# A linear-attention layer's two programs run as one, with the experts' weight pieces dealt out by step

## The chip, the cores and the metric

One core of a Trainium2 chip. The time is the device's microseconds for the whole kernel (two layers); the lower the better. Beside it stands one execution taken by the hardware profiler, whose span and rows are quoted here. VectorE is DVE in the rows, ScalarE is ACT, GpSimd is POOL, TensorE is PE (its weight loads PEld), and SP is the engine that issues most transfers.

## The reference, cut to what matters

2 x 1024 tokens of 512 numbers go through attention, a ternary feed-forward layer, a linear-attention layer and 16 experts of which each token takes two, each with a residual and a layer norm. The part that is changed:

```python
q = k = x @ Wqk + bqk
v = silu(x @ Wv + bv); u = silu(x @ Wu + bu)
q, kh, vh = elu(heads(q)), elu(heads(k)), heads(v)
kv  = einsum('bhnd,bhne->bhde', kh, vh)      # over all 1024 rows of a batch
out = einsum('bhnd,bhde->bhne', q, kv)
out = u * layernorm(out, ln_g, ln_b)
x   = layernorm(x + out @ Wo + bo)
logits = x @ gate_w.T                        # of the experts' router
```

An expert has a gate and up weight of 512 x 704 and a down weight of 352 x 512, all float32.

## The kernel before, in words

Tokens are in 16 tiles of 128 rows (`NT`), 8 to a batch (`TB`). Each product is made from float16 high and low halves: three products for one. Each phase is a program of its own, with its own semaphores, and each engine's order in it is written out by hand: `unrolled(n, stages)` takes steps 0, 1, 2, ... and in each step goes through a list of (lag, function) and calls the function for tile step - lag. An engine does its list in order, so a wait in one function holds up all that stand behind it.

`ternary_ffn` (from L1004) runs 18 steps and more: per tile 32 matmuls at L1084 and 32 at L1094, with the hidden rows turned by a transfer (L1062) that SP issues, and it makes the high and low halves of the next layer's weights (L1144, L1210).

`linear_features` (from L1344) makes, per tile, z = x @ (Wqk, Wv, Wu) in three PSUM banks (L1337, bias L1341), exp and two tanh on ScalarE (L1434, L1439), relu, e, v and U on VectorE (L1485 to L1492), one subtraction on GpSimd (L1530), then the key-value product summed in PSUM over a batch (L1411), the turned keys (L1417) and their halves (L1443, L1497). U of all 16 tiles is kept.

`linear_output_and_route` (from L1536) starts when that program is over. Per tile: q (L1602), its statistics and gating on VectorE (L209, L1690, L1694), the root of the variance (L220), the product with U (L1723) and the low half (L1729) on GpSimd, turning (L164, evacuated at L1654), @ Wo in TensorE (L1337 with `out_ps_y`), residual and statistics on VectorE (L1701, L209), root and shift on GpSimd (L1742, L1745), norm and halves (L1659, L1667, L1736), turning again (L1671), and the logits (L1631, L1709).

`ExpertSplit` (from L1239) turns the experts' float32 weights to float16 halves in the chip's memory. A piece is one k-chunk: seven to an expert, four of 128 x 704, two of 128 x 512 and one of 96 x 512. SP loads it (L1275, L1280) to a ring of buffers, ScalarE makes the high half (L1312), VectorE the low half (L1317), SP stores both (L1290). In `linear_features` the ring has six buffers, the transfers run freely (`transfers`), and the halves of 14 experts (98 pieces) are spread evenly over the steps (`spread`). `linear_output_and_route` takes the last two experts and seven pieces of the shared one, in a ring of four.

Of the kernel before, what the change touches and what calls it, by code (L numbers as in the profile page):

```python
# [1004 lines left out]
def ternary_ffn(nc, m, d):  # L1005
# [8 lines left out]
    with Phase(nc, "ffn") as f:  # L1014
# [27 lines left out]
        ht_in = [[f.sem(f"ht_in{u}{part}") for part in range(2)] for u in range(2)]  # L1042

        with f.block() as block:  # L1044
            @block.sync
            def _(sp):
# [54 lines left out]
            def _(act):  # L1101
# [39 lines left out]
                def next_high(t):  # L1141
# [5 lines left out]
                                      (4, of_layer(h_norm)), (1, of_layer(next_high))])  # L1147

            @block.vector
            def _(dve):  # L1150
# [56 lines left out]
                def next_low(t):  # L1207
# [7 lines left out]
                                      (1, of_layer(x_norm)), (1, of_layer(next_low))])  # L1215
# [19 lines left out]
LIN_EXPERTS = 14  # L1235


class ExpertSplit:
# [54 lines left out]
    def transfers(self, sp):  # L1293

        lag = self.ring - 2
        for i in range(self.count + lag):
            if i < self.count:
                self.load(sp, i)
            if i >= lag:
                self.store(sp, i - lag)  # L1300

# [18 lines left out]
    def spread(self, fn, eng, tiles, later=0):  # L1320


        def until(t):
            return self.count if t == tiles else max(0, t * self.count // tiles - later)

        def at(t):
            if t < tiles:
                for i in range(until(t), until(t + 1)):
                    fn(eng, i)
        return at  # L1330
# [13 lines left out]
def linear_features(nc, m, d):  # L1344

    with Phase(nc, "lin") as f:
# [4 lines left out]
        ps_x = [f.ps(f"ps_x{u}", [P, 2, KC, P], F16) for u in range(2)]  # L1356
        ps_z = [f.ps(f"ps_z{n}", [P, D], F32) for n in range(3)]
        ps_kv = [f.ps(f"ps_kv{b}", [P, KC, P], F32) for b in range(B)]
        ps_k = f.ps("ps_k", [P, KC, P], F32)
        brow = m.U[0:LO_ROW + 1, NT - 4:NT, :]  # L1360
# [6 lines left out]
        split = ExpertSplit(f, m, d, 6, 0, LIN_EXPERTS, 0)  # L1367
        with f.block() as block:
            @block.sync
            def _(sp):  # L1370
                sp.wait_ge(b_zero, 1)
                for i, n in enumerate(("bqk", "bv", "bu", "bo")):
                    sp.dma_start(brow[0:LO_ROW + 1:LO_ROW, i, :], d[f"L1_attn_{n}"][None, :].to_broadcast([2, D])).then_inc(b_in, 16)
                split.transfers(sp)
                for i, n in enumerate(("ln_g", "ln_b")):
                    sp.dma_start(m.ln_gb[:, i, :], d[f"L1_attn_{n}"][None, :].to_broadcast([P, D])).then_inc(m.gb_in, 16)
                split.wait_stored(sp)

            @block.tensor
            def _(pe):  # L1380
                def xt(t):
# [4 lines left out]
                    after(pe, xt_evac, t - 1 - AHEAD)  # L1386
                    transpose_parts(pe, ps_x[u], x2[u], m).then_inc(xt_done, 1)

                def z(t):
                    u = t % 2  # L1390
                    after(pe, xt_evac, t + 1 - AHEAD)
                    if t == 0:
                        for n in range(3):
                            weighed(pe, m, ps_z[n][:, :], n, xT[u])
                        pe.wait_ge(ones_done, 1)
                        pe.wait_ge(bl_done, 1)
                        for n in range(3):
                            biased(pe, m, ps_z[n][:, :], n).then_inc(z_done, 1)
                        return
                    for n, sem in enumerate((relu_done, v_done, u_done)):  # L1400
                        after(pe, sem, t)
                        weighed(pe, m, ps_z[n][:, :], n, xT[u])
                        biased(pe, m, ps_z[n][:, :], n).then_inc(z_done, 1)

                def kv(t):
                    u = t % 2
                    pe.wait_ge(k_done, t + 1)
                    pe.wait_ge(v_done, t + 1)
                    for g in range(KC):
                        s = slice(g * P, (g + 1) * P)  # L1410
                        last = pe.matmul(ps_kv[t // TB][:, g, :], relu[u][:, s], tanh[u][:, 0, s],  # L1411
# [8 lines left out]
                unrolled(NT, [(1, xt), (2, z), (3, kv)])  # L1420

            @block.scalar
            def _(act):
# [6 lines left out]
                def nonlinear(t):  # L1430
                    u = t % 2
                    after(act, k_done, t - 1)
                    act.wait_ge(z_done, t * 3 + 1)
                    act.activation(e[u][:, :], ps_z[0][:, :], ACT.Exp, scale=1.0 / WS).then_inc(e_done, 1)  # L1434
                    after(act, u_done, t - 1)
                    after(act, kv_done, t - 1)
                    for n in range(2):
                        act.wait_ge(z_done, t * 3 + 2 + n)
                        act.activation(tanh[u][:, n, :], ps_z[1 + n][:, :], ACT.Tanh, scale=0.5 / WS).then_inc(tanh_done, 1)  # L1439

                def kt_hi(t):
                    act.wait_ge(kt_done, t + 1)
                    act.activation(m.kT[:, 0, :, t * P:(t + 1) * P], ps_k[:, :, :], ACT.Copy).then_inc(kth_done, 1)  # L1443

                def kv_hi(t):
# [4 lines left out]
                    for a in range(4):  # L1450
                        s = slice(a * DL, (a + 1) * DL)
                        act.activation(m.kv[s, t // TB, 0, :, s], ps_kv[t // TB][s, :, s], ACT.Copy,
                                       scale=KV_SCALE / (2 * WS)).then_inc(kvh_done, 1)

                def biases(t):
                    if t == 0:
# [3 lines left out]
                unrolled(NT, [(0, lambda t: xhi(t + 1)), (1, biases), (2, nonlinear), (3, kt_hi), (3, kv_hi),  # L1460
                              (1, split.spread(split.high, act, NT, 3))])

            @block.vector
            def _(dve):
                dve.memset(m.kv[:, :, :, :, :], 0.0).then_inc(zero_done, 1)

                def biases(t):
                    if t == 0:
                        dve.wait_ge(bh_done, 1)
                        dve.scalar_tensor_tensor(m.bias[low_row, :, :], m.U[low_row, NT - 4:NT, :], WS, m.bias[low_row, :, :],  # L1470
# [1044 lines left out]
```

## Time and profile before

| | |
|---|---|
| median of 3 runs | 1739.52 us (1738.38 to 1745.71) |
| the profiled execution: its time, its span | 1740.19 us, 1738.4 us |
| busy share: PE, DVE, ACT, POOL | 91%, 68%, 54%, 33% |
| mean granted clock of TensorE | 0.973 |
| ternary layer ends, features start | 906.9 us into the span |
| features end, output starts | 1099 us |
| output ends, the experts' program starts | 1211 us |

Busy shares are averages over stages with different limits. The stage in question is the stretch from 907 to 1211 us; a wait of an engine counts where nothing else hides it. Idle time is printed in brackets behind a row, with what released the engine.

### The profile page before, as it was taken

To read this page: it belongs to the slowest core of one execution; us is meant where nothing else is said; L and a number is where in the kernel's file an instruction comes from. 1 tells how busy PE (TensorE), PEld (TensorE's weight loads), DVE (VectorE), ACT (ScalarE), POOL (GpSimd) and SP (SyncE) were. 2 spreads that over 40 slices of the span, in tenths; PEclk is the share of its full clock that TensorE was granted. 3 is DMA by queue.
4 is the path that set the end of the run, shared out by engine and by line. 5 is a ranking of instruction groups with operands and counts; after the bars stand their busy time and mean duration, and the time that the engine had idled before them with its cause. 6 is when DMAs were issued, how large, how long until landed. Compare 5 with 4: busy or idle time off the path is not lost. (4 is left out here: it accounts for less than half of the span.)

```text
span 1738.4 us, 33564 instructions
## 1 busy us (share of the span) xinstructions
PE 1585.8 (91%) x12554; PEld 803.7 (46%) x12554; DVE 1176.6 (68%) x2074; ACT 933.9 (54%) x1641; POOL 576.3 (33%) x583
## 2 busy tenths in 40 slices
PE   6899999889999997999978999687898899999997
PEld 3533333364333342444434444454555556666564
DVE  4599998468999955899857777895723243333387
ACT  5756777345677754767736665476223333333332
POOL 4556575161000021223321111595271111111265
PEclk9999999899999998999999999798999999999999
DMA  7323332000000002655638999551151764456344
GB/s 248 137 39 56 76 68 48 2 1 2 14 2 2 2 2 63 125 109 110 106 73 315 353 334 363 179 182 61 55 101 51 276 226 167 154 179 219 105 126 134
DMA packets 177842, 211.42 MB, mean 122 GB/s; under 512 B 114203, under 2 KB 117625, under 8 KB 175505
## 3 DMA queue, kind: packets, MB, share of 16 engines
q1 hardware_dynamic: 170336, 188.54, 36.3%
q0 software_dynamic: 7344, 20.73, 4.4%
q8 instruction: 101, 1.65, 0.4%
q14 instruction: 61, 0.49, 0.1%
HBM read 193.33 MB, written 56.40 MB: 144 GB/s over the span
## 5 line engine op out<-in xcount | busy, mean ns | idle before, releaser
L717 ACT ACTIVATE layer_scratch<-layer_banks 128x512 f32<-128x512 f32 x576 | 312.5, 596 | 128.7 <-PE layer_banks L609 127.2
L828 DVE TENSOR_REDUCE layer_mx<-layer_banks 128x2 f32<-128x1024 f32 (+3 forms) x304 | 339.2, 1156 | 24.0 <-PE layer_banks L587 20.6
L2218 PE MATMUL sparse_ps_g<-wgate,sparse_xT 128*128 128x352 f16 x1128 | 185.5, 315 | 1.6 <-DVE sparse_xT L2296 1.6
L624 PE MATMUL layer_banks<-layer_scratch,V 128*32 128x256 f32 x2304 | 174.5, 389 | 0.8 <-ACT layer_scratch L725 0.8
L1337 PE MATMUL lin_ps_z<-arena,early 128*128 128x512 f16 x576 | 134.5, 384 | 6.8 <-PEq L1044 3.5
L2218 PEld LDWEIGHTS sparse_ps_g<-wgate,sparse_xT 128*128 128x128 f16 x1128 | 108.9, 98 | 63.1 <-DVE sparse_xT L2296 2.0
L2302 DVE SCALAR_TENSOR_TENSOR sparse_hid<-sparse_th,sparse_ps_g 128x352 f32<-128x352 f32 x47 | 24.5, 521 | 155.8 <-ACT sparse_th L2263 155.8
L2329 POOL DMA_INDIRECT xg<-x_d,token x45 | 42.6, 947 | 252.5 <-PE sparse_ps_x L2208 252.5
L1094 PE MATMUL ffn_ps_y<-wprojT,ffn_hT 128*128 128x512 f16 x512 | 116.1, 386 | 8.0 <-DMA ffn_hT<-ffn_h 8.0
L1084 PE MATMUL ffn_ps_fc<-wfcT,early 128*128 128x512 f16 x512 | 114.7, 383 | 5.7 <-PEq L950 3.4
L587 PE MATMUL layer_banks<-KT,arena 64*128 64x512 f16 (+3 forms) x768 | 113.8, 330 | 6.5 <-DVE layer_mx L828 6.3
L609 PE MATMUL layer_banks<-arena,KT 64*128 64x256 f16 x1152 | 111.9, 273 | 6.1 <-ACT layer_scratch L717 4.3
L2250 PE MATMUL sparse_ps_y<-wdown,sparse_hT 128*128 128x512 f16 (+1 forms) x423 | 100.6, 383 | 10.4 <-ACT sparse_hT L2276 9.1
L1317 DVE SCALAR_TENSOR_TENSOR lin_sp_parts<-lin_sp_raw,lin_sp_parts 128x704 f16<-128x704 f32 (+2 forms) x98 | 78.6, 840 | 36.6 <-ACT lin_sp_parts L1312 36.5
L1312 ACT ACTIVATE lin_sp_parts<-lin_sp_raw 128x704 f16<-128x704 f32 (+2 forms) x98 | 67.3, 718 | 55.8 <-DMA lin_sp_raw<-in_L_ffn_w_gate_up_dram 40.2
L1337 PEld LDWEIGHTS lin_ps_z<-arena,early 128*128 128x128 f16 x576 | 53.6, 99 | 73.2 <-issue 13.5
L220 POOL TENSOR_TENSOR ffn_lnr_rstd<-ffn_lnr_var,minus_half 128x1 f32<-128x1 f32 x16 | 36.7, 2297 | 141.7 <-DVE ffn_lnr_var L215 141.7
L1094 PEld LDWEIGHTS ffn_ps_y<-wprojT,ffn_hT 128*128 128x128 f16 x512 | 50.6, 99 | 71.4 <-DVE ffn_r L1199 5.5
L1084 PEld LDWEIGHTS ffn_ps_fc<-wfcT,early 128*128 128x128 f16 x512 | 50.2, 98 | 68.5 <-issue 6.4
L942 POOL TENSOR_TENSOR layer_turned_rows<-O,layer_turned_rows 128x512 f16<-128x512 f32 x16 | 18.5, 1158 | 186.7 <-ACT layer_turned_rows L730 186.7
L624 PEld LDWEIGHTS layer_banks<-layer_scratch,V 128*32 128x32 f32 x2304 | 49.6, 108 | 63.8 <-issue 35.1
L609 PEld LDWEIGHTS layer_banks<-arena,KT 64*128 64x128 f16 x1152 | 39.0, 94 | 86.1 <-issue 42.0
(305 smaller groups left out, 3129.4 us busy)
## 6 DMA issues: line engine op xcount, KB each, us to landing
wgate<-gate_d SPq DMA_DIRECT2D x47, 1408.0 KB
wdown<-down_d SPq DMA_DIRECT2D x47, 768.0 KB
lin_sp_raw<-in_L_ffn_w_gate_up_dram SPq DMA_DIRECT2D x56, 352.0 KB, 5.0
gate_d<-lin_sp_parts SPq DMA_DIRECT2D x56, 352.0 KB, 4.8
y_d<-y SPq DMA_DIRECT2D x47, 256.0 KB
down_d<-lin_sp_parts SPq DMA_DIRECT2D x42, 256.0 KB, 4.7
lin_sp_raw<-in_L_ffn_w_down_dram SPq DMA_DIRECT2D x28, 256.0 KB, 5.3
wfcT<-in_L_ffn_w_fc_dram SPq DMA_DIRECT2D x8, 512.0 KB, 7.6
```

Source lines behind the costliest of these rows:

```text
L587: last = pe.matmul(slots[par][:, h, :], QT[s, pair + h, qt * P:(qt + 1) * P], KT[s, (pair + h) // 2, c * 512:c * 512 + n], start=not diago ...
L609: last = pe.matmul(ps_t[:, (2 * g + par) % 3, i, :], KT[s, j, kt * P:(kt + 1) * P], QT[s, 2 * j:2 * j + 2, qt * P:(qt + 1) * P], start=kt ...
L624: last = pe.matmul(ps_o[32 * jj:32 * jj + 32, 256 * half:256 * half + 256], V[:, kt, 4 * jg + jj, :], prob[(2 * q + jj // 2) % 4][:, half, ...
L717: act.activation(prob[g % 4][:, par, :, :], ps_t[:, (2 * g + par) % 3, :, :], ACT.Exp, scale=HD ** -0.5).then_inc(exp_done, 1)
L828: dve.tensor_reduce(mx[x % 2][:, c, :, at:at + per], ps_s[:, 2 * (r % 2):2 * (r % 2) + 2, 0:per * n].rearrange("p e (h k) -> p e h k", k=n ...
L1084: last = pe.matmul(ps_fc[n][:, :], xT[u][:, part, k, :], m.wfcT[:, k, n * D:(n + 1) * D], start=(k == 0 and part == 0), stop=(k == KC - 1 ...
L1094: last = pe.matmul(ps_y[u][:, :], hT[u][:, part, k, :], m.wprojT[:, k, :], start=(k == 0 and part == 0), stop=(k == NK - 1 and part == 1))
L1312: act.activation(self.part(i, 0), self.raw[u][0:rows, 0:width], ACT.Copy, scale=WS).then_inc(self.hi_done, 1)
L1317: dve.scalar_tensor_tensor(self.part(i, 1), self.raw[i % self.ring][0:rows, 0:width], WS, self.part(i, 0), ALU.mult, ALU.subtract).then_in ...
L1337: pe.matmul(out, xT[:, a, k, :], m.w1[:, i, b, k, :], start=(k == 0 and n == 0), stop=False)
L2218: last = pe.matmul(ps_g[u][n][rows, :], xT[u][:, a, k, rows], w, start=(k == 0 and i == 0), stop=(k == KC - 1 and i == 2), skip_group_chec ...
L2250: last = pe.matmul(ps_y[u][rows, :], hT[u][0:size, a, k, rows], w, start=(k == 0 and i == 0), stop=(k == 2 and i == 2), skip_group_check=L ...
```

## The change

`linear_features` and `linear_output_and_route` become one program, `linear_layer`. A tile's output steps follow its features by `OUT_LAG` = 11 steps and more: features' z at lag 2, key-value product at lag 3; q at lag 11, product with U and gating 12, low half 13, turning 14, Wo 15, norm 16, second turning 18, logits 19. So steps 0 to 10 hold features alone, 11 to 18 both, 19 to 34 output alone. U is a ring of 11 tiles. All eight PSUM banks are handed out by hand: z has two (was three), the turned x one (was two), q, the turned w, y and the logits one each.

The pieces are no longer spread evenly. Expert 0 is split in the ternary layer, one piece in each second step, in a ring of three. The 112 others are split in the merged program, in a ring of four, by `in_part`: steps 1 to 10 have four each, at four fixed places of a step; steps 11 to 18 have eight, two at each place; from step 19 on two, at the last two places. SP loads piece i+4 right behind the store of piece i.

```diff
 # ternary_ffn
+        split = ExpertSplit(f, m, d, 3, 0, FFN_EXPERTS, 0)
 # SP
-                unrolled(NT + AHEAD, [(0, of_layer(next_layer)), (3, xt), (5, of_layer(ht(0))), (5, of_layer(ht(1)))])
+                unrolled(NT + AHEAD, [(0, of_layer(next_layer)), (3, xt), (3, split.every_second(split.load, sp)),
+                                      (5, of_layer(ht(0))), (5, of_layer(ht(1))), (7, split.every_second(split.store, sp))])
 # ScalarE and VectorE: last in each step
+                                      (5, split.every_second(split.high, act))])
+                                      (1, of_layer(x_norm)), (1, of_layer(next_low)), (5, split.every_second(split.low, dve))])
...
-LIN_EXPERTS = 14
+FFN_EXPERTS = 1
+OUT_LAG = 11
+URING = OUT_LAG
...
+    def in_part(self, s, part):
+        one, last = 4 * (OUT_LAG - 1), OUT_LAG + TB
+        if 1 <= s < OUT_LAG:
+            at, size = 4 * (s - 1) + part, 1
+        elif OUT_LAG <= s < last:
+            at, size = one + 8 * (s - OUT_LAG) + 2 * part, 2
+        elif last <= s and part >= 2:
+            at, size = one + 8 * TB + 2 * (s - last) + part - 2, 1
+        else:
+            at, size = 0, 0
+        return range(at, min(at + size, self.count))
...
 # linear_layer
+        banks = f.ps("banks", [P, 8, 512], F32)
+        turns = lambda n: banks[:, n, :].bitcast(F16).rearrange("p (a k c) -> p a k c", a=2, k=KC)
+        ps_x, ps_w = turns(0), turns(6)
+        ps_z = lambda t, i: banks[:, 1 + (3 * t + i) % 2, :]
...
-        split = ExpertSplit(f, m, d, 6, 0, LIN_EXPERTS, 0)
+        split = ExpertSplit(f, m, d, 4, FFN_EXPERTS, NE - FFN_EXPERTS, 1)
...
 # SP
+                def pieces(s):
+                    for i in split.in_step(s):
+                        split.store(sp, i)
+                        if i + split.ring < split.count:
+                            split.load(sp, i + split.ring)
+
+                unrolled(NT + Q + 7, [(0, lambda s: rows(s - Q - 6)), (0, pieces)])
...
 # TensorE, z of the three weights one by one
+                        if i == 0:
+                            after(pe, xt_evac, t + 1 - AHEAD)
+                            after(pe, v_done, t)
+                        if i == 1:
+                            after(pe, u_done, t)
+                        if i == 2:
+                            pe.wait_ge(relu_done, t + 1)
...
-                unrolled(NT, [(1, xt), (2, z), (3, kv)])
+                unrolled(NT, [(1, xt), (Q + 3, wt), (2, z(0)), (Q, q), (2, z(1)), (Q + 4, wo), (2, z(2)), (3, kv), (3, router),
+                              (Q + 8, logit), (Q + 7, ot)])
...
 # ScalarE
+                unrolled(NT + Q + 8, [(0, of(lambda t: xhi(t + 1), 0)), (0, of(biases, 1)), (0, of(wevac, Q + 3)), (0, of(whi, Q + 2)), (0, of(exps, 2)),
+                                      (0, pieces(0)), (0, of(norm, Q + 5)), (0, of(ohi, Q + 5)), (0, pieces(1)), (0, of(tanhs, 2)),
+                                      (0, of(kt_hi, 3)), (0, of(kv_hi, 3)), (0, of(router, 4)), (0, pieces(2)), (0, of(oevac, Q + 7)), (0, pieces(3))])
 # VectorE
+                unrolled(NT + Q + 9, [(0, of(gating, Q + 1)), (0, of(xevac, 1)), (0, of(biases, 1)), (0, of(keys, 2)), (0, pieces(0)),
+                                      (0, of(stats, Q)), (0, pieces(1)), (0, of(values, 2)), (0, of(kt_lo, 3)), (0, of(kv_lo, 3)),
+                                      (0, of(router, 4)), (0, of(residual, Q + 4)), (0, pieces(2)), (0, of(levac, Q + 8)), (0, pieces(3))])
 # GpSimd
-                unrolled(NT, [(0, xlo), (2, minus_one)])
-                unrolled(NT, [(7, xlo), (2, wlo), (5, root_r), (1, product), (0, lambda t: ln_q.root(pool, t, t % 2))])
+                unrolled(NT, [(0, xlo), (Q + 5, root_r), (Q + 6, olo), (Q + 2, wlo), (Q + 1, product), (2, minus_one),
+                              (Q, lambda t: ln_q.root(pool, t, t % 2))])
```

## Rows read from the trace of the kernel before

**Rows 1.** Stretches from:to, length; each engine's busy us; granted clock, DMA share, GB/s.

```profile
core 0: us, PE busy (x) PEld busy (x) DVE busy (x) ACT busy (x) POOL busy (x), PEclk, DMA share, GB/s
931.00:1086.00 155.00, 154.35 (x829) 76.16 (x827) 119.71 (x173) 93.33 (x156) 27.96 (x26) 1.00 0.96 347
...
1131.08:1172.35 41.27, 35.66 (x386) 21.70 (x384) 39.71 (x100) 31.50 (x44) 40.21 (x43) 1.00 0.55 183
```

**Rows 2.** Timeline of TensorE, two tiles of features: start, duration, operation.

```profile
954.15 1.16 PE L1411 MATMUL lin_ps_kv<-lin_tanh,lin_relu 128*128 128x128 f32 x8
...
965.06 1.16 PE L1411 MATMUL lin_ps_kv<-lin_tanh,lin_relu 128*128 128x128 f32 x8
```

**Rows 3.** Timeline of TensorE: first product, seam, output tile 8, last logits, the experts' program.

```profile
906.92 7.93 PE L1337 MATMUL lin_ps_z<-arena,early 128*128 128x512 f16 x36 [3.46 <-PEq L1044]
...
1093.25 2.08 PE L1411 MATMUL lin_ps_kv<-lin_tanh,lin_relu 128*128 128x128 f32 x8 [6.21 <-POOL lin_relu L1530]
...
1099.01 2.00 PE L1602 MATMUL out_ps_q<-kv,xT 128*128 128x128 f16 x24 [2.83 <-PEq L1368]
...
1131.08 0.83 PE L1602 MATMUL out_ps_q<-kv,xT 128*128 128x128 f16 x12
...
1207.99 1.01 PE L164 MATMUL out_ps_x<-ident,out_x 128*128 128x128 f16 x8 [0.79 <-ACT xT L1671]
...
1210.12 0.59 PE L1631 MATMUL out_ps_l<-out_gT,xT 128*128 128x16 f16 x16 [0.70 <-ACT xT L1671]
1211.24 9.59 PE L156 MATMUL disp_ps_g<-arena,xT 128*128 128x352 f16 x48 [0.53 <-PEq L1571]
```

**Rows 4.** Who ScalarE waited for, 931 to 1086 us: total, times, longest.

```profile
ACT lin_sp_parts L1312 <- DMA lin_sp_raw<-in_L_ffn_w_gate_up_dram: 34.3, 28, 3.4
```

**Rows 5.** DMA issues of the whole kernel: count, KB each, median us to landing.

```profile
lin_sp_raw<-in_L_ffn_w_gate_up_dram SPq DMA_DIRECT2D x56, 352.0 KB, 5.0
...
lin_sp_raw<-in_L_ffn_w_down_dram SPq DMA_DIRECT2D x28, 256.0 KB, 5.3
...
out_sp_raw<-in_L_ffn_w_gate_up_dram SPq DMA_DIRECT2D x8, 352.0 KB, 3.8
...
ffn_hT<-ffn_h SPq DMA_TRANSPOSE x32, 4.4
```

**Rows 6.** A stretch of the ternary layer, columns as in rows 1.

```profile
822.00:850.00 28.00, 28.00 (x131) 12.64 (x130) 25.07 (x49) 20.00 (x29) 7.72 (x7) 1.00 0.55 95
```

**Rows 7.** Timeline of the ternary layer: SP's turn, VectorE after it, TensorE's use.

```profile
851.56 4.89 SPq L1062 DMA_TRANSPOSE ffn_hT<-ffn_h  x2
...
857.88 2.29 DVE L990 TENSOR_REDUCE ffn_qh_g<-ffn_hn 128x1 f32<-128x2048 f32 x1 [2.90 <-ACT ffn_hn L1138]
...
861.44 7.07 PE L1094 MATMUL ffn_ps_y<-wprojT,ffn_hT 128*128 128x512 f16 x32
```

**Rows 8.** Timeline of the features' start, ScalarE and TensorE.

```profile
916.92 0.79 ACT L1312 ACTIVATE lin_sp_parts<-lin_sp_raw 128x704 f16<-128x704 f32 x1 [0.66 <-DMA lin_sp_raw<-in_L_ffn_w_gate_up_dram]
...
918.25 1.28 ACT L1434 ACT_TABLE_LOAD   x1
...
920.92 5.13 PE L1337 MATMUL lin_ps_z<-arena,early 128*128 128x512 f16 x12 [2.70 <-DVE lin_relu L1485]
...
926.31 2.76 PE L1337 MATMUL lin_ps_z<-arena,early 128*128 128x512 f16 x12
```

**Rows 9.** The slow product's stretch, columns as in rows 1.

```profile
920.90:926.00 5.10, 5.08 (x13) 1.66 (x13) 5.10 (x7) 3.30 (x6) 2.15 (x2) 0.52 0.71 280
```

**Rows 10.** Low halves (L1317) alone, in two stretches: VectorE busy (count), clock, DMA, GB/s.

```profile
core 0: us, DVE busy (x), PEclk, DMA share, GB/s
931.00:1086.00 155.00, 67.74 (x85) 1.00 0.96 347
1131.00:1172.00 41.00, 11.61 (x9) 1.00 0.55 183
```

**Rows 11.** GpSimd's groups, 1131.08 to 1197.3 us: busy us, mean ns.

```profile
L220 POOL TENSOR_TENSOR out_lnq_rstd<-out_lnq_var,minus_half 128x1 f32<-128x1 f32 x9 | 10.2, 1133 | 0.0
L1742 POOL TENSOR_TENSOR out_lnr_rstd<-out_lnr_var,minus_half 128x1 f32<-128x1 f32 x12 | 10.0, 835 | 3.3 <-DVE out_lnr_var L215 3.3
```

**Rows 12.** Timeline of GpSimd: a short root.

```profile
1142.54 0.55 POOL L1742 TENSOR_TENSOR out_lnr_rstd<-out_lnr_var,minus_half 128x1 f32<-128x1 f32 x1
```

More of the change, by code:

```diff
@@ L1291, in store @@
                      self.parts[i % self.ring][:, 0:2 * width]).then_inc(self.stored[i % self.ring], 16)
[L1293 to L1300, printed above, removed]
     def wait_stored(self, sp):
@@ L1318, in low, with in_step, every_second @@
                                  ALU.mult, ALU.subtract).then_inc(self.lo_done, 1)
-    def spread(self, fn, eng, tiles, later=0):
-        def until(t):
-            return self.count if t == tiles else max(0, t * self.count // tiles - later)
+    def in_part(self, s, part):
[9 more added lines that the diff above has]
+        return range(at, min(at + size, self.count))
+    def in_step(self, s):
+        return [i for part in range(4) for i in self.in_part(s, part)]
+    def every_second(self, fn, eng):
         def at(t):
-            if t < tiles:
-                for i in range(until(t), until(t + 1)):
-                    fn(eng, i)
+            if t % 2 == 0 and t // 2 < self.count:
+                fn(eng, t // 2)
         return at
@@ L1418, in kv, with router, q @@
                     last.then_inc(kt_done, 1)
-                unrolled(NT, [(1, xt), (2, z), (3, kv)])
+                def router(t):
+                    if t == 0:
+                        pe.wait_ge(gate_in, 16)
+                        for k in range(KC):
+                            last = pe.transpose(ps_gate[:, k, :], gate[:, k * P:(k + 1) * P], m.ident[0:NE, 0:NE])
+                        last.then_inc(g_done, 1)
+                def q(t):
+                    if t % TB == 0:
+                        pe.wait_ge(kvl_done, 4 * (t // TB + 1))
+                    pe.wait_ge(ktl_done, t + 1)
+                    after(pe, n1_done, t)
+                    s = slice(t * P, (t + 1) * P)
+                    for g in range(KC):
+                        for n, (a, c) in enumerate(((0, 0), (0, 1), (1, 0))):
+                            last = pe.matmul(ps_q[:, g, :], m.kT[:, a, g, s], m.kv[:, t // TB, c, g, :], start=(n == 0), stop=(n == 2))
+                    last.then_inc(q_done, 1)
@@ new lines, in ot, with logit @@
+                def ot(t):
+                    pe.wait_ge(ol_done, t + 1)
+                    if t == 0:
+                        pe.wait_ge(xt_evac, NT - AHEAD)
+                    after(pe, ot_evac, t)
+                    transpose_parts(pe, ps_x, o2[t % 2], m).then_inc(ot_done, 1)
+                def logit(t):
+                    if t == 0:
+                        pe.wait_ge(ktl_done, NT)
+                    pe.wait_ge(ot_evac, t + 1)
+                    after(pe, l_evac, t)
+                    s = slice(t * P, (t + 1) * P)
+                    for k in range(KC):
+                        for n, (a, c) in enumerate(((0, 0), (0, 1), (1, 0), (1, 1))):
+                            last = pe.matmul(ps_l, m.xT3[:, a, k, s], gT[:, c, k, :],
+                                             start=(k == 0 and n == 0), stop=(k == KC - 1 and n == 3))
+                    last.then_inc(l_done, 1)
```

380 lines of the change are left out of this document (171 added, 209 removed).

## The prediction

> **What bounds the kernel now.** I began with the page: TensorE is busy 91% of 1738.4 us, and the chain that ended last only tells of the final microseconds, so the stage that the change touches has to be read by itself. The table by stretch comes first [rows 1]. In the features, 931 to 1086 us, TensorE is busy 154.35 of 155 us and the transfers' share is 0.96 at 347 GB/s: two limits at once. From the product of tile 8 to that of tile 15 in the output program (1131.08 to 1172.35, seven tiles) VectorE is busy 39.71 of 41.27 us and GpSimd 40.21, TensorE only 35.66. The timeline of TensorE gives the cadence: a tile of features each 10.91 us, the start of its key-value product [rows 2]; a tile of output each 41.27/7 = 5.90 us; and the seam: TensorE waits 6.21 us for GpSimd ahead of the last tile's product at 1093.25, and starts the first product of the output program at 1099.01; the experts' program starts at 1211.24 [rows 3]. At full cadence the two programs would keep TensorE busy for 16 x (10.91 + 35.66/7 = 5.09) = 256 us, and they take 906.92 to 1211.24 = 304.3. So 48 us are idle or slow, and that is what one merged program can fight for.
>
> But the merged program must also carry the experts' pieces, and there the limits change. Before, 6.1 pieces go beside each tile of features. ScalarE waits 34.3 us for the wide ones in that stretch [rows 4], which costs nothing, since TensorE never waits. A load takes 5.0 us to land there, 3.8 in the output program [rows 5].
>
> **Part 1, ternary layer.** Seven pieces (expert 0) go beside it, one each second step: seven loads and seven stores on SP's queue, seven copies on ScalarE (0.8 us) and seven low halves on VectorE (0.8 to 0.9). SP's load waits for the low half of three pieces ago, its store for one issued two steps earlier: neither is late. Behind them on the queue stand the turns of the hidden rows; VectorE is busy about 25 of 28 us here [rows 6], so the low half delays that chain by under 1 us per two steps, some 4 us by the seventh. The cover is there: the first turn is issued at 851.56, takes 4.4 us to land and is wanted at 861.44, 5.5 us of slack; afterwards VectorE idles 2.90 us per tile [rows 5, 7], which lets it catch up before the last tiles, whose turns TensorE does wait for. Cost 0; if the cover fails, up to +4.
>
> **Part 2, the start.** Only two banks hold z now, so tile 0's third product waits for the first's relu, and ScalarE takes four pieces ahead of the exponential, not three. Before: third piece at 916.92, table load 918.25, relu done about 920.9, tile 1 at 920.92 with a product of 5.13 us at a granted clock of 0.52 (the 1.2 GHz level), as good as a start at 926.31 - 3.0 = 923.3 [rows 8, 9]. After: the fourth piece ends about 919.1; copy 0.6, table 1.28, exponential 0.6, relu 0.7 give 922.3; the third product at that clock 5.1, bias 0.4, transposes 0.45: tile 1 at 928.3. **+5.0 us.** Steps 2 to 10 then run as before: four pieces a step, and each two-bank wait has 3.0 us (one product) for 1.3 us of exponential and relu. Step 11 starts at 928.3 + 8 x 10.91 = 1015.6.
>
> **Part 3, steps 11 to 18.** These decide. Output starts beside features, and each step has eight pieces. Four resources, per step:
> TensorE: 10.91, +0.7 for q, up to +4.2 from step 15 on: 11.6 to 15.1; about 6.5 in step 18.
> Transfers: an expert is 4 x 704 + 2 x 512 + 448 KB, in and out (its last piece has 96 rows), so a piece is 627 KB and eight are 5.02 MB: 14.5 us at 347 GB/s, 13.9 if the share 0.96 went to 1.
> The ring, now of four buffers: load i+4 is issued when low half i is done. Issues 0.6, landing 5.0, copy 0.8, low half 0.8 to 1.0: 7.4 us for four pieces, 14.8 for eight. Before, six buffers.
> VectorE: its features cost (119.71 - 67.74)/14.2 = 3.66 us per tile and its output (39.71 - 11.61)/7 = 4.0; a low half costs 67.74/85 = 0.80 us beside the features but 11.61/9 = 1.29 beside the output [rows 1, 10]. The operation is the same; what differs is GpSimd, busy 18% and 97%. At about half in steps 15 to 17 I take 0.99 by proportion: 3.66 + 4.0 + 7.9 = 15.6, over the 96% that it reached, 16.2 us.
> So step 11 (four pieces landed already) 12.5, steps 12 to 14 14.8 each, 15 to 17 16.2 each, step 18 14.8: 120.3. Tile 8's product starts at 1015.6 + 120.3 = 1135.9; before 1131.08: **+4.8**, the start's +5.0 within it. The seam's 6.2 us and the slow filling behind it are won, and lost again: TensorE stands 1 to 8 us in each of these steps.
>
> The Trainium skill, SBUF — State Buffer, section Who interferes with whom, says a VectorE instruction with two SBUF inputs contends with a GpSimd one that reads SBUF, and that the lock is held for a whole instruction. The low half reads the raw piece and its high half, both in SBUF, so 0.80 against 1.29 agrees in direction; by that rule the dearer rate could hold in all eight steps, which is rival C.
>
> **Part 4, the tail.** Before, 1131.08 to 1211.24 is 80.2 us [rows 3]. After, steps 19 to 22 have two pieces each: VectorE 4.0 + 2 x 1.29 = 6.6, over 0.96 is 6.9 against 5.90, +4.0. Then no pieces: VectorE falls to 4.0 and GpSimd binds; its one-column roots take 1.13 and 0.84 us where the shortest shown is 0.55 [rows 11, 12], so I take 5.4 for seven steps, -3.5 (bounds 0 and -6). The residual and the logits sit one step earlier: one short step of 1210.12 - 1207.99 = 2.1 less. Product, residual, turned rows and logits have one bank each instead of two for some; each waits on an evacuation done one step before, price 0, bound +0.5 a step for 16 steps. **Tail 78.6, -1.6.**
>
> **The sum:** 4.8 - 1.6 = +3.2 on the profiled execution's 1740.19: 1743.4. Its median of three is 0.7 lower, so I forecast 1743 us: no change. About 0.5%, 8.7 us, is what can be told apart here.
>
> **Rivals.**
> A, faster: the merged steps flow at the bare limits. Landing falls below 5.0 because fewer transfers are in flight (3.8 is on record at 183 GB/s), low halves stay at 0.80. Steps 12 to 14 and 18 at 13.9, 15 to 17 at TensorE's 15.1, step 11 at 12: 112.9, 7.4 less. The start costs 3 instead of 5, and the tail is 3 to 6 shorter: 1743.4 - 12.4 = 1731, down to 1728. For it: ScalarE has slack everywhere; against it, transfers at 0.96 are already a wall, so 8 pieces can't go below 13.9.
> B, slower: the ring. Two pieces sit at four fixed places of each step, behind operations that wait for TensorE, and a buffer that lands must wait for its place. If a half turn takes 8.4 in place of 7.4, steps 12 to 14 and 18 take 16.8 and 15 to 17, where VectorE adds to it, 18: 134 against 120.3, so 1757. It decides from a half turn of 7.8 up: 14 half turns at 0.35 more are the 4.8 us between the forecast and +8.7.
> C, slower: the low halves at 1.29 in all of steps 11 to 18: 3.66 + 4.0 + 10.3 = 18.0, over 0.96 is 18.7 in steps 15 to 17 (+2.5 each); 16.2 over 0.96 in 12 to 14 (+2 each); +1.5 in the two others: +15, 1758. It decides from a mean of 1.1 in the heavy steps. Against it: GpSimd has 7.7 us of work in a step of 16 and can't be in the way of each.
> D, the change does less than it says: the last pieces or the seam's 12 us only move to another place, say the ternary layer's end: +4 to +6, 1748.
>
> **Chances.** Forecast 0.43 (own range 1734 to 1752), A 0.26, B 0.12, C 0.13, D 0.06. A, which ends at or below 1731, gives 0.21 of faster by over 8.7 us, the rest of it is within; B, C, half of D and the upper edge of the forecast give 0.33 slower; 0.46 is left for no change. The range reaches to A and to just past C, widened at both ends by the tail's bounds: 1724 to 1762.
>
> **What would show it.** Right: TensorE gapless at 10.91 until about 1015, then steps of 14 to 16 us with gaps put down to VectorE's relu or v, and ScalarE waiting for raw pieces; VectorE over 95% busy from 1028 to 1136; the ternary end still at 906 to 908. Part 2 is wrong if tile 1 starts before 926. Part 3 is wrong if the eight heavy steps take under 112 or over 130 us; low halves by their mean (0.8, 1.0 or 1.3) tell A from C, and landing by its median tells A from B. Part 4 is wrong if late output tiles take more than 5.9 us. The whole is wrong if the last logits end before 1203 or after 1224.

## The result and the profile after

The changed kernel takes 1757.49 us (median of 6, 1756.62 to 1759.62) against 1739.83 (1734.47 to 1745.71) for the kernel before: ratio 1.0106, 95% interval 1.0090 to 1.0122. It is slower by 1.1%. The forecast was 1743 us with a range of 1724 to 1762. That range holds the result; the forecast's own range, 1734 to 1752, does not. The profiled execution has a span of 1757.3 us and a mean granted clock of 0.968.

TensorE's timeline of the changed kernel shows where the 19 us enter (start us, us, engine, line, operation, count, idle before it):

```profile
888.01 8.75 PE L1097 MATMUL ffn_ps_y<-wprojT,ffn_hT 128*128 128x512 f16 x32 [4.29 <-DMA ffn_hT<-ffn_h]
900.20 9.89 PE L1097 MATMUL ffn_ps_y<-wprojT,ffn_hT 128*128 128x512 f16 x32 [3.44 <-DMA ffn_hT<-ffn_h]
...
913.55 6.62 PE L1346 MATMUL lin_banks<-arena,early 128*128 128x512 f16 x24 [3.46 <-PEq L1045]
923.58 1.01 PE L1350 MATMUL lin_banks<-bias,ones_row 33*128 33x512 f16 x2 [3.40 <-DVE bias L1621]
928.74 4.97 PE L1346 MATMUL lin_banks<-arena,early 128*128 128x512 f16 x12 [4.16 <-DVE lin_relu L1636]
...
934.42 0.81 PE L1346 MATMUL lin_banks<-arena,early 128*128 128x512 f16 x3
...
1149.18 1.46 PE L1490 MATMUL lin_banks<-kv,xT 128*128 128x128 f16 x12 [7.19 <-DVE kv L1662]
...
1157.41 0.83 PE L1490 MATMUL lin_banks<-kv,xT 128*128 128x128 f16 x12 [0.18 <-DVE lin_w L1679]
...
1230.59 8.80 PE L156 MATMUL disp_ps_g<-arena,xT 128*128 128x352 f16 x48 [0.54 <-PEq L1398]
```

The features start at 913.55 in place of 906.92 [rows 3]: +6.6. Of that 1.5 us lie ahead of anything that the change touches: the ternary layer's first product starts at 668.03, before at 666.52. Tile 1 comes 20.87 us after the features' start (934.42 - 913.55); before it took 16.4. Output tile 8 starts at 1149.18 in place of 1131.08, the experts' program at 1230.59 in place of 1211.24: +19.35 in all, and the span grew by 18.9. Nothing of note changed ahead of 668 or behind 1231 us.

Three stretches of the changed kernel by engine (columns as in rows 1), steps 3 to 10, steps 11 to 18, and the output behind them up to 1205 us, of which the last low half starts at 1180.4:

```profile
931.00:1022.16 91.16, 91.16 (x494) 44.86 (x491) 63.15 (x85) 44.34 (x76) 27.10 (x17) 0.99 0.74 240
1022.16:1149.18 127.02, 104.92 (x617) 52.98 (x614) 110.91 (x179) 74.36 (x122) 46.48 (x40) 0.93 0.90 304
1149.18:1205.00 55.82, 47.32 (x466) 27.48 (x467) 44.10 (x123) 39.55 (x55) 44.49 (x51) 0.95 0.36 126
```

The first is as tight as before [rows 1], with transfers at 0.74 instead of 0.96: room for more pieces is there and unused. In the second three are high and none is full: VectorE 87%, transfers 0.90, TensorE 83%. The low halves alone (L1314) in the same stretch, and the wide and narrow loads over the whole kernel:

```profile
1022.16:1149.18 127.02, 57.04 (x62) 0.93 0.90 304
```

```profile
lin_sp_raw<-in_L_ffn_w_gate_up_dram SPq DMA_DIRECT2D x60, 352.0 KB, 4.4
...
lin_sp_raw<-in_L_ffn_w_down_dram SPq DMA_DIRECT2D x30, 256.0 KB, 4.1
```

57.04/62 = 0.92 us a low half, and 4.4 us to landing. TensorE's waits, 905 to 1240 us of the changed kernel (total us, times, longest):

```profile
PE lin_banks L1346 <- DVE lin_tanh L1644: 9.3, 4, 4.3
PE lin_banks L1490 <- DVE kv L1662: 7.2, 1, 7.2
PE lin_banks L164 <- POOL lin_w L1745: 6.0, 7, 1.5
PE lin_banks L1346 <- DVE lin_relu L1636: 6.0, 3, 4.2
PE lin_banks L1521 <- ACT xT L1599: 5.6, 4, 1.7
```

The four waits for v (L1644) lie in steps 11 to 18, which are called heavy below because they have eight pieces each; the one for the halves of the key-value product is the longest of all.

### The profile page after: what moved, and what is told of

Its sections match the earlier page's. It is cut to its first block and busy times, and to the rows that moved or that the text cites. A ratio compares the mean times of both kernels' runs of the same rounds, so it can differ in the third digit from the quotient of the medians.

```text
span 1757.3 us, 33578 instructions
## 1 busy us (share of the span) xinstructions
PE 1595.4 (91%) x12554; PEld 802.4 (46%) x12554; DVE 1184.5 (67%) x2074; ACT 933.3 (53%) x1641; POOL 588.1 (33%) x583
## 5 line engine op out<-in xcount | busy, mean ns | idle before, releaser
L1346 PE MATMUL lin_banks<-arena,early 128*128 128x512 f16 x576 | 139.9, 395 | 18.8 <-DVE lin_tanh L1644 9.3
L2235 PEld LDWEIGHTS sparse_ps_g<-wgate,sparse_xT 128*128 128x128 f16 x1128 | 108.4, 98 | 62.2 <-DVE sparse_xT L2313 2.0
L609 PE MATMUL layer_banks<-arena,KT 64*128 64x256 f16 x1152 | 111.9, 273 | 6.1 <-ACT layer_scratch L717 4.3
L2267 PE MATMUL sparse_ps_y<-wdown,sparse_hT 128*128 128x512 f16 (+1 forms) x423 | 102.6, 389 | 8.6 <-ACT sparse_hT L2293 8.6
L1314 DVE SCALAR_TENSOR_TENSOR lin_sp_parts<-lin_sp_raw,lin_sp_parts 128x704 f16<-128x704 f32 (+2 forms) x105 | 96.3, 952 | 14.1 <-ACT lin_sp_parts L1309 13.7
L1309 ACT ACTIVATE lin_sp_parts<-lin_sp_raw 128x704 f16<-128x704 f32 (+2 forms) x105 | 73.0, 717 | 52.8 <-DMA lin_sp_raw<-in_L_ffn_w_gate_up_dram 34.1
L1346 PEld LDWEIGHTS lin_banks<-arena,early 128*128 128x128 f16 x576 | 55.0, 101 | 88.4 <-issue 27.7
L1097 PEld LDWEIGHTS ffn_ps_y<-wprojT,ffn_hT 128*128 128x128 f16 x512 | 50.6, 100 | 76.4 <-issue 12.8
```

What stands on the lines that cost most here:

```text
L609: last = pe.matmul(ps_t[:, (2 * g + par) % 3, i, :], KT[s, j, kt * P:(kt + 1) * P], QT[s, 2 * j:2 * j + 2, qt * P:(qt + 1) * P], start=kt ...
L1097: last = pe.matmul(ps_y[u][:, :], hT[u][:, part, k, :], m.wprojT[:, k, :], start=(k == 0 and part == 0), stop=(k == NK - 1 and part == 1))
L1309: act.activation(self.part(i, 0), self.raw[u][0:rows, 0:width], ACT.Copy, scale=WS).then_inc(self.hi_done, 1)
L1314: dve.scalar_tensor_tensor(self.part(i, 1), self.raw[i % self.ring][0:rows, 0:width], WS, self.part(i, 0), ALU.mult, ALU.subtract).then_in ...
L1346: pe.matmul(out, xT[:, a, k, :], m.w1[:, i, b, k, :], start=(k == 0 and n == 0), stop=False)
L2235: last = pe.matmul(ps_g[u][n][rows, :], xT[u][:, a, k, rows], w, start=(k == 0 and i == 0), stop=(k == KC - 1 and i == 2), skip_group_chec ...
```

## The experiments

Single profiled executions differ by up to 6.4 us in where the ternary layer starts (663.49 to 669.91), so the table goes by stage: A from the ternary layer's first product to the features' first, B to the start of step 11 (tile 9's z), C to the product of output tile 8, D to the experts' program. Before, B and C are counted from the same events in the two old programs. Where the edits leave a stage alone, it still differs between the traces: A 243.8 to 245.5, B 108.0 to 108.6, C 126.6 to 127.4, D 81.4 to 83.5 (after, e1, e2, e4). Differences of that size say nothing. The times of e1 to e8 are single executions; e9 to e11 are medians of 9 to 12.

| kernel | A | B | C | D | one time or median | the kernel before beside it |
|---|---|---|---|---|---|---|
| before | 240.4 | 103.7 | 120.5 | 80.2 | 1739.8 | |
| after | 245.5 | 108.6 | 127.0 | 81.4 | 1757.5 | 1739.8 |
| e1 no pieces in the ternary layer | 240.4 | 108.4 | 126.6 | 83.5 | 1751.0 | 1734.4 |
| e2 its low halves twice | 248.2 | 108.0 | 127.4 | 83.0 | 1761.6 | 1734.4 |
| e3 step 18's pieces at its last two places | 244.1 | 108.1 | 120.5 | 90.7 | 1758.9 | 1734.4 |
| e4 no pieces in step 1 | 244.1 | 104.7 | 126.8 | 82.7 | 1751.8 | 1734.4 |
| e5 thin low halves | 245.4 | 108.3 | 117.7 | 81.1 | 1741.1 | 1742.8 |
| e6 thin loads | 243.8 | 108.1 | 121.3 | 83.0 | 1754.9 | 1742.8 |
| e7 ring of three | 244.3 | 114.2 | 144.9 | 84.4 | 1781.6 | 1742.8 |
| e8 even dealing | 244.0 | 111.9 | 102.4 | 86.8 | 1739.2 | 1742.8 |
| e9 even, step 1 clear | 245.4 | 105.2 | 103.1 | 88.6 | 1735.1 | 1737.6 |
| e10 e9, no pieces in the ternary layer | 240.7 | 105.3 | 102.6 | 92.4 | 1734.6 | 1737.6 |
| e11 e10, six a step | 240.7 | 108.8 | 103.7 | 87.7 | 1732.9 | 1737.6 |

Most edits replace `in_part` by a table of how many pieces each of a step's four places takes; the table that equals the change is

```python
def DEALT(s):
    if 1 <= s < OUT_LAG:            return (1, 1, 1, 1)
    if OUT_LAG <= s < OUT_LAG + TB: return (2, 2, 2, 2)
    return (0, 0, 1, 1) if s >= OUT_LAG + TB else (0, 0, 0, 0)
```

**e1, the ternary layer alone.**

```diff
-FFN_EXPERTS = 1
+FFN_EXPERTS = 0
+    if 4 <= s < OUT_LAG: return (2, 1, 1, 1)
```

> Expert 0 is split in the merged program again: its seven pieces go one each into steps 4 to 10, beside features, and nothing stands beside the ternary layer. If the ternary layer's 6.6 us come from the pieces beside it, its end goes back from 913.55 to about 907 us; in the merged program steps 4 to 10 stay at 10.91 us, since transfers there move only 240 GB/s, and the total falls by 6 to 7 us. Rival: the layer's end moved for another reason (a shift of the profile or of the attention before it), and the end stays at 912 to 914.

Stage A is 240.4, as before; with pieces it is 243.8 to 245.5 in the eight kernels that have the change's ternary layer: the seven pieces cost 3.4 to 5.1 us. They cost nothing beside the features, where B stays at 108.4. The four stages together fall by 3.7 us and not by 6 to 7, since D comes out 2.1 longer. TensorE's last two tiles of the ternary layer in e1, then the last in the kernel before (timelines):

```profile
882.85 7.07 PE L1097 MATMUL ffn_ps_y<-wprojT,ffn_hT 128*128 128x512 f16 x32 [0.30 <-DMA ffn_hT<-ffn_h]
894.92 8.75 PE L1097 MATMUL ffn_ps_y<-wprojT,ffn_hT 128*128 128x512 f16 x32 [5.00 <-DMA ffn_hT<-ffn_h]
...
894.71 8.75 PE L1094 MATMUL ffn_ps_y<-wprojT,ffn_hT 128*128 128x512 f16 x32 [5.03 <-DMA ffn_hT<-ffn_h]
```

Without pieces the long wait for turned rows is there once, 5.0 us, at the last tile; the change has 4.29 and 3.44, at the last two. Measured from the layer's first product, the last product starts at 228.2 us in the kernel before and at 232.2 in the change, 4.0 later; and it takes 9.89 us at a granted clock of 0.71, before 8.75 at 0.80. 4.0 and 1.1 are the 5.1 of stage A.

**e2, each of those low halves twice** (the second result is written to a spare tile and used by nothing):

```diff
+        if self.ring == 3:
+            dve.scalar_tensor_tensor(self.again[0:rows, 0:512], self.raw[...][0:rows, 0:512], WS, self.part(i, 0)[:, 0:512],
+                                     ALU.mult, ALU.subtract).then_inc(self.again_done, 1)
```

> Beside the ternary layer each low half is made a second time, 512 columns into an unused PSUM bank (0.7 us, seven times, 4.8 us of VectorE); transfers and ScalarE as in the changed kernel. If VectorE's chain carries the cost, the last turned rows and so the end of the layer come 4 to 5 us later, about 918. Rival, the transfers and their collisions with the turns: the end stays at 913 to 914.

The added work is 7 x 0.68 = 4.8 us of VectorE. The last product of the layer starts 236.3 us after the first, in the change at 232.2: 4.1 us later, most of what was added. A grows only by 2.7, because that last product takes 8.52 us (granted clock 0.83) and not 9.89. So VectorE's chain passes such work on to the end of the layer. VectorE in the changed kernel around the seventh piece (tile 13) with ScalarE's norm ahead of it, then the last tile's reduction (L990) before and after (timelines):

```profile
862.08 2.09 ACT L1141 ACTIVATE ffn_hn<-ffn_h,ffn_shift,ffn_rstd 128x2048 f32<-128x2048 f32 x1 [1.71 <-POOL ffn_shift L1231]
864.73 0.69 DVE L1314 SCALAR_TENSOR_TENSOR ffn_sp_parts<-ffn_sp_raw,ffn_sp_parts 96x512 f16<-96x512 f32 x1 [3.42 <-ACT ffn_sp_parts L1309]
865.34 2.27 DVE L990 TENSOR_REDUCE ffn_qh_g<-ffn_hn 128x1 f32<-128x2048 f32 x1
...
884.19 2.29 DVE L990 TENSOR_REDUCE ffn_qh_g<-ffn_hn 128x1 f32<-128x2048 f32 x1 [2.90 <-ACT ffn_hn L1138]
...
889.73 2.29 DVE L990 TENSOR_REDUCE ffn_qh_g<-ffn_hn 128x1 f32<-128x2048 f32 x1 [2.90 <-ACT ffn_hn L1141]
```

The reduction (L990, once a tile) stands behind the low half in VectorE's list. Measured from the layer's first product, it is later than before by 0.9 us behind each wide low half and by 0.6 behind each narrow one, 4.8 us behind six. At tile 13 it starts at 865.34, before at 857.88 [rows 7]: 6.0 us later. The wait of 3.42 us is mostly one that was there without pieces (2.90 us, for ScalarE's norm, which ends at about 864.2 here); the seventh piece adds its copy of 0.6 on ScalarE and its low half of 0.6. In the last two tiles 1.9 us are caught up: 889.73 against 884.19 is 4.0 us later. That is the delay of the last product.

**e3, the key-value halves first.** Step 18's eight pieces all go to the step's last two places, behind the halves of the second batch's key-value product:

```diff
+    if s == OUT_LAG + TB - 1: return (0, 0, 4, 4)
```

> Only step 18 is dealt anew: its eight pieces stand at the third and fourth place, behind the halves of the second batch's key-value product, not two at each place. If q of tile 8 waits because those halves are queued behind four pieces, its wait falls from 7.2 us to 1 or 2 and the product starts at about 1143 to 1145 instead of 1149.2; the pieces themselves then end later, and 2 or 3 us are given back in steps 19 on: total 3 to 5 us less. Rival, the pieces' own rate is the bound and the wait is only where it shows: product and total stay within 1.5 us.

TensorE at this place in e3 (timeline):

```profile
1140.76 0.84 PE L1492 MATMUL lin_banks<-kv,xT 128*128 128x128 f16 x12 [2.39 <-DVE kv L1664]
...
1156.57 1.03 PE L164 MATMUL lin_banks<-ident,lin_w 128*128 128x128 f16 x8 [9.29 <-POOL lin_w L1747]
```

The wait falls from 7.19 to 2.39 and tile 8's product comes 6.5 us sooner in its stage (C 120.5), more than the 4 to 6 expected. Then TensorE stands 9.29 us for the next gated rows, behind the same pieces: C and D together are 211.2 against 208.4 to 210.4 in the kernels that leave step 18 alone (after, e1, e2, e4). Nothing is won in all, where 3 to 5 us were expected. The wait for the key-value halves is only the place where the cost of eight pieces shows.

**e4, no pieces in step 1:**

```diff
+    if s == 1:       return (0, 0, 0, 0)
+    if 3 <= s <= 6:  return (2, 1, 1, 1)
```

> Step 1 has no pieces; four steps from 3 to 6 have five. If the start's loss comes from the four pieces ahead of the exponential on ScalarE, relu of tile 0 ends about 3 us sooner and tile 1 starts at about 931 instead of 934.4. Rival: two banks and the bias are the whole cost (third product behind relu); then tile 1 moves by less than 1 us.

The start of e4 in TensorE's timeline:

```profile
922.58 1.01 PE L1354 MATMUL lin_banks<-bias,ones_row 33*128 33x512 f16 x2 [4.62 <-DVE bias L1625]
924.58 4.27 PE L1350 MATMUL lin_banks<-arena,early 128*128 128x512 f16 x12 [0.99 <-DVE lin_relu L1640]
```

The wait for relu is 0.99 instead of 4.16 and B falls by 3.3 to 3.9, of which 0.7 is the third product itself (4.27 us at a granted clock of 0.64, in the change 4.97 at 0.55). The pieces ahead of the exponential are most of the start's cost.

**e5, thin low halves in steps 11 to 18** (one column in place of 704 or 512, so those low halves are missing from the split weights):

```diff
+        if self.ring == 4 and 40 <= i < 104:
+            dve.scalar_tensor_tensor(self.part(i, 1)[:, 0:1], self.raw[...][0:rows, 0:1], WS, self.part(i, 0)[:, 0:1], ...)
+            return
```

> In steps 11 to 18 the low halves are one column wide (the output then lacks those halves), so some 57 us of VectorE go; loads, stores and the high halves stay. If VectorE binds these steps, they fall to TensorE's own 11.6 to 15.1 us, 100 to 105 us from step 11 to tile 8's product instead of 127. If the ring and the transfers bind, each piece is only 0.9 us shorter in its ring of four (7.4 to 6.5 us a turn) and the stretch stays over 112.

**e6, thin loads in steps 11 to 18** (32 columns of a piece are loaded, the rest of the buffer holds an older piece; the stores stay whole):

```diff
+        if self.ring == 4 and 44 <= i < 104:
+            sp.dma_start(raw[:, 0:32], <the same rows>[..., 0:32]).then_inc(sem, 16)
+            return
```

> In steps 11 to 18 a load brings 32 columns in place of 704 or 512 (the halves are then made of stale rows); stores, high and low halves keep their size. Half of the transfers' bytes go and a load lands in 2 to 3 us. If transfers or the ring bind, the stretch from step 11 to tile 8's product falls from 127 to 108 to 115 us, with the waits for raw pieces gone on ScalarE. If VectorE binds, it stays over 120.

Stage C of e5 and of e6 by engine, columns as in rows 1:

```profile
1017.60:1135.30 117.70, 101.19 (x617) 52.29 (x614) 71.30 (x178) 74.47 (x122) 36.14 (x40) 0.95 0.93 328
```

```profile
1021.90:1143.20 121.30, 102.04 (x617) 52.30 (x614) 113.61 (x179) 74.08 (x124) 50.95 (x40) 0.95 0.51 181
```

With VectorE relieved (71.3 of 117.7 us busy) the transfers stand at 0.93 and the stretch takes 117.7: 64 pieces at 1.84 us, four of them (one turn of the ring) in 7.36. With the transfers relieved (0.51) VectorE is busy 113.6 of 121.3, 94%. By e5's expectation VectorE is not the limit, by e6's it is: relieving either wins 6 to 9 us and neither brings the 100 to 105 us that were expected of TensorE's work alone. So there are two limits close to each other, and the ring of four ties them together: a piece that lands late leaves VectorE idle, and a late low half starts the next load late. Neither run takes its limit away wholly (in e6 ScalarE still waits 28.5 us for raw pieces, against the expectation), and no run relieves both.

**e7, a ring of three:**

```diff
-        split = ExpertSplit(f, m, d, 4, FFN_EXPERTS, NE - FFN_EXPERTS, 1)
+        split = ExpertSplit(f, m, d, 3, FFN_EXPERTS, NE - FFN_EXPERTS, 1)
```

> Ring of three buffers in the merged program instead of four. If a turn of the ring is what spaces the pieces, eight pieces take 8/3 turns of some 6.5 to 7.4 us, 17 to 20 us a step: the stretch grows from 127 to 140 to 155 us. If VectorE or the transfers' rate bind and the ring has room, it grows by less than 6 us.

C grows by 18 us, as expected for a ring that spaces the pieces; B grows by 5.6, all in the start (TensorE waits 9.65 us for relu). ScalarE's waits for raw pieces in 1024 to 1170 us of e7:

```profile
ACT lin_sp_parts L1309 <- DMA lin_sp_raw<-in_L_ffn_w_gate_up_dram: 40.4, 28, 3.9
ACT lin_sp_parts L1309 <- DMA lin_sp_raw<-in_L_ffn_w_down_dram: 29.4, 18, 4.0
```

69.8 us in all; the change has 46.8 from 1022 to 1149 us (32.3 and 14.5). The ring's depth bears on the heavy steps. Five and six buffers, which would show the other direction, were not tried.

**e8, the same 112 pieces dealt more evenly:**

```diff
+    if 1 <= s < OUT_LAG:                return (2, 1, 1, 1)
+    if OUT_LAG <= s < OUT_LAG + TB - 1: return (2, 1, 2, 1)
+    if s >= OUT_LAG + TB - 1:           return (0, 0, 1, 1)
```

> The 112 pieces dealt more evenly: five in each of steps 1 to 10, six in 11 to 17, two in step 18 and from 19 on. If the eight pieces a step are what slows steps 11 to 18, these come down to TensorE's pace, 12 to 15.1 us each and about 100 to 105 us to tile 8's product instead of 127; steps 2 to 10 stay at 10.91. Nine output steps with two pieces instead of four cost about 1 us each, +5: total 15 to 20 us less than the changed kernel. Rival, the merged step costs more for another reason (single banks, shared ports): the stretch stays over 115.

Its stretch C, columns as in rows 1:

```profile
1021.20:1123.60 102.40, 98.12 (x617) 51.60 (x614) 93.34 (x160) 61.44 (x105) 50.73 (x40) 1.00 0.84 282
```

102.4 in place of 127.0. TensorE has 617 instructions in both but is busy 98.12 us at a granted clock of 1.00, in the change 104.92 at 0.93: its own work is 6.8 us shorter by the clock alone. How much of the 24.6 us won that makes up was not told apart, since TensorE stands idle for 22 us of the change's stretch. What the moved pieces cost elsewhere: B +3.3, all in the start (TensorE waits 8.17 us for relu, with five pieces in step 1), and D +5.4. The sum falls by 16 us, and the time is 1739.2 beside 1742.8.

**e9 to e11, the repairs together.** e9 is e8 with step 1 clear; e10 also has `FFN_EXPERTS = 0`; e11 also has six pieces (2, 1, 2, 1) in steps 3 to 10:

```diff
 # e9, e10
-    if 1 <= s < OUT_LAG:                return (2, 1, 1, 1)
+    if 2 <= s < OUT_LAG:                return (2, 1, 1, 1)
 # e11
+    if s == 2:                          return (2, 1, 1, 1)
+    if 3 <= s < OUT_LAG + TB - 1:       return (2, 1, 2, 1)
```

> The even dealing with step 1 free of pieces: 5 pieces in steps 2 to 10, 6 in 11 to 17, then two a step from 18 on (25 left over). If the two repairs add up, the start gives back 7.3 us (tile 1's first product 24.2 us after the first in the even version, 16.9 with the start clear) and 2.5 more output steps with pieces cost 1.15 each (6.85 against 5.7): 1739 - 7.3 + 2.9 = about 1735, some 8 under the kernel before. If the output steps only wait for VectorE's own work, the extra pieces are free: 1732. If the time is 1739 or more, the start's gain was taken back in the later steps.

1735.11 us, ratio to the kernel before 0.9982 (0.9972 to 0.9992). The start gives back 6.7 (B 105.2 against 111.9), and C and D together take 2.5 for the five more pieces of the tail (191.7 against 189.2); the expectation said 7.3 and 2.9. The second is hardly above what D differs by without cause.

> As e9, and the ternary layer without its seven pieces (119 in the merged program, 32 of them left over at step 18). The ternary layer gives back 5.1 us, the seven pieces cost 3.5 more output steps at 1.15: 1 us less than e9, about 1734. If pieces in the late steps are free: 5 less than e9.

1734.62 us, ratio 0.9983 (0.9971 to 0.9994). A gives back 4.7, and C and D together take 3.3 for seven more pieces. Both are near the size expected (5.1 and 4.0); by their times e9 and e10 can't be told apart.

> As e10, with six pieces instead of five in steps 3 to 10, as many as the kernel before had beside a tile, but in a ring of four: 24 left over at step 18. If VectorE's and TensorE's work alone set those steps they stay at 10.91 and the time is e10's less 4 steps of 1.15, about 1729. If the ring turns too slowly for six (four buffers in 7.3 us, so landing, two copies and a place in 7.3), steps 3 to 10 take 11.3 to 12 and the time is 1732 to 1738.

1732.86 us, ratio 0.9970 (0.9958 to 0.9983). Steps 3 to 10 of e10, then of e11:

```profile
923.90:1011.70 87.80, 87.78 (x477) 43.55 (x478) 72.61 (x90) 47.49 (x81) 27.08 (x16) 1.00 0.86 289
```

```profile
925.90:1017.20 91.30, 88.50 (x477) 43.65 (x478) 73.48 (x97) 52.52 (x88) 24.27 (x16) 1.00 0.94 321
```

Five pieces a step leave TensorE gapless, six in a ring of four don't: +3.5 us over eight steps, the rival's lower end. The stretches behind it win 3.6 (C and D 191.4 against 195.0), so in the traces nothing is gained over e10 (e11's trace is of its slowest execution, 1738.87 us, but the excess lies outside these stages), and the 1.8 us between their medians lie within their intervals. All three beat the kernel before by 0.2 to 0.3%. By way of the kernel before, e11 beats the changed one by 1.3% (0.9970/1.0106 = 0.987).

## Why the prediction was right or wrong

Predicted was +3.2 us, measured between the traces +19.35 at the experts' program (+17.7 between the medians). By its own sign the whole was wrong: the last logits end at 1230.1, and after 1224 was named. The missing 16.1, from front to back:

- **Ahead of the change, +1.5.** The ternary layer started later; that start differs by up to 6.4 us between the profiles here.
- **Part 1, ternary layer, 0 against +5.1.** Here the prediction failed: in the cover, not in the drift. It saw a drift of "some 4 us by the seventh"; measured are 4.8 behind six pieces and 6.0 behind the seventh. It covered it twice, with 5.5 us of slack at the first turn and with VectorE's 2.90 us of idling a tile. But at the last tile TensorE already waits 5.03 us for its turned rows in the kernel before, as the prediction itself noted, so slack at tile 12 covers nothing at tile 15. And the idling is a wait for ScalarE at the end of the same chain, which comes late with it: it gave back 1.9 us, and 4.0 reached the last product. The last product's lower clock added 1.1. The bound of +4 was a little short.
- **Part 2, the start, +5.0 against +4.5.** Right, in size and in mechanism (e4: 3.3 to 3.9 of it goes with the pieces). Steps 3 to 10 take 10.91 each with free transfers, as forecast; step 2 took 11.4, and step 11 starts within 0.1 us of the forecast place behind the features' start.
- **Part 3, 120.3 against 127.0.** Steps 11 to 17 take 107.35 (12.8, 16.1, 15.2, 16.5, 16.7, 14.85, 15.2) against 105.5. The sum is right to 2%, in part by luck: steps 12 to 14 are 3.3 over (47.7 against 44.4), 15 to 17 are 1.8 under (46.8 against 48.6). The low halves' mean of 0.92 lies below the 0.99 taken. What failed is step 18, 19.7 against 14.8: it was priced as eight pieces that flow, but the halves of the second batch's key-value product stand in the list behind the first four of them on both engines, and the next product needs them; TensorE waits 7.19 us. e3 shows that the order within the step only chooses who waits. The reasoning on single resources also missed how they join: VectorE is at 87%, not "over 95%", and e5 and e6 take 118 and 121 where the change takes 127. The sum also took TensorE's work at full clock. In step 15 (1082.71 to 1099.43) TensorE is busy all of the 16.72 us, at a granted clock of 0.90, where its work was priced at 15.1 or less: there its own pace was the limit.
- **Part 4, the tail, 78.6 against 81.4.** Four such steps were priced at 6.9. Five have low halves in them, since VectorE still had four pieces of step 18 to do (12 low halves behind 1149.18, not 8): a first one of 8.2 and four of 6.80 to 7.05. That 6.9 was hit by luck. It was priced as VectorE 96% busy with low halves of 1.29 us; the low halves take 0.79 on average (9.48/12), and over the four steps from tile 9's product to tile 13's the trace has (columns as in rows 1):

```profile
1157.41:1184.96 27.55, 21.26 (x229) 12.67 (x229) 22.06 (x61) 21.04 (x31) 23.54 (x25) 1.00 0.41 149
```

VectorE is 80% busy there, GpSimd 85%, and TensorE waits 5.3 us for GpSimd's low half of the gated rows (L1745). The steps behind, without pieces, take 5.96 and 5.70 instead of 5.4. GpSimd's roots do fall to 0.55 us there, as guessed. Seven tiles take 47.4 against 43.8, the drain takes 0.8 less than thought.

1.5 + 5.1 - 0.1 + 6.7 + 2.8 = 16.0, which is the 16.1 but for rounding.

The rivals. **A** fell: steps 16 and 17 do come down to its 15.1 us, but steps 12 to 14 take 15.2 to 16.5 where it had 13.9, though landing did fall to 4.4 (4.7 in the heavy stretch). **B** named the mechanism nearest to what e5 to e7 show: steps 12 to 17 take 7.9 us for four pieces, its "half turn" (94.55/12), just past its deciding point of 7.8, but not its 8.4. (The gap that this point was worked out from is 8.7 - 3.2 = 5.5 us, not 4.8; the point stays at 7.8.) Its time of 1757 was hit by luck, by a sum of four smaller things, and so was C's 1758. **C** fell: 0.92, where 1.1 would decide. **D** named the ternary layer's end and +4 to +6 for it; that happened, on top of the forecast's own terms and not in place of them. The error common to all is that they were laid out as alternatives: the ternary layer's +4 and the tail's waits for single banks (up to +8) stood in the text as bounds, and the sum took nothing for either, while it credited the tail with a gain.

On the prediction's sentence from the Trainium skill (SBUF — State Buffer, section Who interferes with whom): by that rule the dearer low half could hold in all heavy steps. The trace does not bear that out (0.92 us on average, GpSimd busy 46.48 of 127.02 us).

## What to carry to other kernels

When background work is dealt out to the steps of a merged program, deal it by the room that each step has: the same 112 pieces cost 16 us less in the linear layer at 5, 6 and 2 a step than at 4, 8 and 2, because a step that is at two limits at once, coupled by a small ring, takes longer than with either of them relieved. Give no background work to a pipeline's first step (e4: 3.3 to 3.9 us). Moving it to the end of the step in which a value for all later tiles is finished won nothing (e3); giving that step less was only tried together with the even dealing. Before pricing a drift at nothing because there is slack, look at the last iteration of the loop: if the main engine already waits there, there is none.

## What the runs showed of the hardware

VectorE and GpSimd lengthen each other more evenly than the low halves' 1.29 had suggested. GpSimd, then VectorE, in the changed kernel (timeline):

```profile
1058.83 1.62 POOL L1733 TENSOR_TENSOR lin_relu<-lin_e,ones 128x512 f32<-128x512 f32 x1 [0.65 <-DVE lin_e L1638]
...
1073.67 1.27 POOL L1739 TENSOR_TENSOR lin_w<-U,lin_w 128x512 f32<-128x512 f32 x1
```

```profile
1058.67 0.88 DVE L1314 SCALAR_TENSOR_TENSOR lin_sp_parts<-lin_sp_raw,lin_sp_parts 128x704 f16<-128x704 f32 x1
...
1073.72 1.76 DVE L1638 SCALAR_TENSOR_TENSOR lin_e<-lin_e,lin_relu 128x512 f32<-128x512 f32 x1
```

At 1058.7 VectorE is first: its low half takes 0.88 as ever, and GpSimd's subtraction 1.62, where it took 1.04 in the features before. At 1073.7 GpSimd is first by 0.05 us: its product takes its usual 1.27, and VectorE's e takes 1.76 instead of 0.69. So in both the one that comes second pays. It pays 0.58 and 1.07 us, somewhat less than the 0.72 and 1.22 for which the first still ran. The Trainium skill, SBUF — State Buffer, section Who interferes with whom, says the same: "Issue order, not op shape, decides who blocks." On average over stretch C, e rose from 0.69 to 1.26 us and GpSimd's x low part (L1728) from 1.16 to 1.88. No run here took this overlap away, so its share of the 19 us is not known.

TensorE's granted clock was lower in the stretches in which it had stood longer. Two rows of the changed kernel (timeline) show one such place: behind a wait of 4.31 us the product takes 5.26 us at a granted clock of 0.52 (the 1.2 GHz level), and the next one 2.75 at 1.00 (2.4 GHz).

```profile
1051.04 5.26 PE L1346 MATMUL lin_banks<-arena,early 128*128 128x512 f16 x12 [4.31 <-DVE lin_tanh L1644]
...
1057.22 2.75 PE L1346 MATMUL lin_banks<-arena,early 128*128 128x512 f16 x12
```

Over stretch C the mean granted clock was 1.00 in e8, 0.93 in the change and 0.90 in e7, and TensorE's busy time for the same 617 instructions 98.12, 104.92 and 109.37 us. A load of 352 KB lands in a median of 4.2 us in e7's stretch C (270 GB/s), in 4.7 in the change's (304) and in 5.5 in e5's (328).
